# A Mamba block with a ternary FFN on one core: where rows load, which engine takes head 1's low weights, and three reordered steps

## What is computed

```python
zxbcdt = jnp.einsum('bld,ed->ble', u, W_in)
dt = jax.nn.softplus(zxbcdt[..., -NHEADS:] + dt_bias)
xBC = jax.nn.silu(xconv)                  # causal convolution over 4 positions of x, B and C
y = (Y_diag + Y_off).reshape(b, l, h, p)  # within a chunk, and from the state before it
yg = (y + x * D) * jax.nn.silu(z)
yn = yg * jax.lax.rsqrt(jnp.mean(yg * yg) + EPS) * norm_w
x = _layernorm(u + jnp.einsum('ble,de->bld', yn, W_out))
scale = jnp.mean(jnp.abs(w)) + EPS        # for W_up, W_gate and W_down
w_q = jnp.clip(jnp.round(w / scale), -1.0, 1.0) * scale
x = _layernorm(x + (silu(x @ w_up_q.T) * (x @ w_gate_q.T)) @ w_down_q.T)
```

## Time and profile before

| what | value |
|---|---|
| median of 3 runs | 1373.71 us (1372.25 to 1374.39) |
| the profiled execution's own time | 1370.55 us |
| its span | 1368.4 us |
| TensorE busy | 1331.5 us, 97% of the span |
| VectorE, ScalarE, GpSimd busy | 1046.1, 785.2 and 666.7 us |
| mean granted clock of TensorE | 0.997 of 2.4 GHz |

### The profile page before, as it was taken

The page is one execution under the profiler, slowest core; times in us unless marked ns, Lnnn a source line. Parts: engine busy times, 40 slices in busy tenths (PEclk is TensorE's granted clock), DMA queues, the critical chain, the costliest instruction groups (busy, mean ns, idle before and its releaser), DMA issues.

```text
span 1368.4 us, 24907 instructions
## 1 busy us (share of the span) xinstructions
PE 1331.5 (97%) x9318; PEld 867.0 (63%) x9318; DVE 1046.1 (76%) x1855; ACT 785.2 (57%) x1561; POOL 666.7 (49%) x640
## 2 busy tenths in 40 slices
PE   8987899999999999999999999999999999999998
PEld 5554455564655656556557767777777777777774
DVE  7985787886878868778786987777777767777675
ACT  6885475782865838748475544454545445454441
POOL 3883265573763836635356534343444435353331
PEclk9999999999999999999999999999999999999999
DMA  7536434362443643524546332223122322222001
GB/s 252 174 109 208 133 119 119 86 177 78 103 134 96 167 111 86 150 90 132 158 120 223 89 114 57 76 63 86 47 63 65 75 67 58 70 62 55 32 28 66
DMA packets 162776, 143.64 MB, mean 105 GB/s; under 512 B 101344, under 2 KB 123232, under 8 KB 161504
## 3 DMA queue, kind: packets, MB, share of 16 engines
q1 hardware_dynamic: 162656, 142.05, 36.2%
HBM read 99.93 MB, written 27.39 MB: 93 GB/s over the span
## 4 chain that ended last, share of the span: by engine, by line
PE 82%; DVE 8%; issue 4%; ACT 2%; POOL 2%; DMA 1%; SPq 0%; POOLq 0%; DVEq 0%; ACTq 0%
PE ring L935 20%; PE ring L1151 15%; PE ring L964 9%; PE p_turn L1131 7%; PE p_y L1131 7%; PE p_st L1131 6%; PE p_seg L1131 6%; PE p_y L1009 3%; PE p_y L1017 2%; PE p_st L999 2%; PE p_turn L989 2%; DVE acc L1831 1%; PE ring L1188 1%; DMA raw<-in_w_in 1%; POOL sq_sum L1643 1%
## 5 line engine op out<-in xcount | busy, mean ns | idle before, releaser
L935 PE MATMUL ring<-u_split,weights 128*128 128x512 f16 x1620 | 373.1, 380 | 0.5 <-DVE x_ch L1836 0.5
L935 PEld LDWEIGHTS ring<-u_split,weights 128*128 128x128 f16 x1620 | 154.3, 98 | 168.7 <-issue 4.1
L1739 POOL TENSOR_TENSOR xdt<-xdt 128x512 f32<-128x512 f32 x64 | 100.8, 1575 | 324.4 <-DVE xdt L2230 324.4
L964 PE MATMUL ring<-w_out,raw 128*128 128x512 f16 x672 | 147.3, 379 | 0.0
L1831 DVE SCALAR_TENSOR_TENSOR acc<-ring,taps,acc 128x511 f32<-128x511 f32 (+2 forms) x192 | 143.7, 749 | 4.5
L964 PEld LDWEIGHTS ring<-w_out,raw 128*128 128x128 f16 x672 | 65.8, 98 | 79.0
L1359 ACT ACTIVATE xdt<-p_turn,dts 128x128 f32<-128x128 f32 x256 | 72.9, 375 | 71.2 <-PE p_turn L989 71.1
L1635 POOL TENSOR_TENSOR raw<-yg,raw 128x512 f16<-128x512 f32 x64 | 78.8, 1232 | 66.0 <-ACT raw L1390 66.0
L1630 POOL TENSOR_TENSOR yg<-y_ch,z_ch 128x512 f32<-128x512 f32 x64 | 81.5, 1275 | 36.8 <-DVE y_ch L1966 36.8
L1368 ACT ACTIVATE p_seg<-cum_rows,cum 128x128 f32<-128x128 f32 x256 | 80.8, 389 | 6.9 <-DVE seg L1944 6.9
L1606 POOL TENSOR_TENSOR rstd<-var_e,exponent 128x1 f32<-128x1 f32 x32 | 19.6, 611 | 124.7 <-DVE var_e L1989 124.7
(11 more groups left out here) (400 smaller groups left out, 3264.2 us busy)
## 6 DMA issues: line engine op xcount, KB each, us to landing
cum_rows<-cum_dram SPq DMA_DIRECT2D x64, 256.0 KB, 4.1
quant<-in_w_ffn SPq DMA_DIRECT2D x24, 512.0 KB, 4.5
quant<-in_w_ffn SPq DMA_DIRECT2D x48, 256.0 KB, 4.7
cum_g<-cum_dram SPq DMA_DIRECT2D x64, 128.0 KB, 4.6
rows<-in_u_tok SPq DMA_DIRECT2D x32, 256.0 KB, 5.1
x_dram<-rows SPq DMA_DIRECT2D x32, 256.0 KB, 2.1
tern_ug<-quant SPq DMA_DIRECT2D x32, 256.0 KB, 3.2
u_raw<-in_u_t SPq DMA_DIRECT2D x7, 1024.0 KB, 7.7
```

The costliest lines, as they stand in the source:

```text
L935: mm = pe.matmul(bank_k[:, :], w_in[:, ws, k, col:col + P], us[:, par, k * T:(k + 1) * T], start=(i == 0), stop=(i == 3 * KD - 1))
L964: mm = pe.matmul(ring[b][:, :], ys[:, h, c * P:(c + 1) * P], w_out[:, ws, h, :], start=(h == 0 and ys is y_hi and ws == 0), stop=(h == H - ...
L1739: pool.tensor_tensor(tile_[:, 1, :, :], tile_[:, 0, :, :], tile_[:, 1, :, :], ALU.mult).then_inc(hid_ok, 1)
```

## The change

Five edits, in the order of the program:

- `POOL_HEADS` now holds head 1 too: its low weights are made by GpSimd, first of all its heads, and no longer by VectorE (`w_lo(2)`). The numbers that the semaphores wait for follow.
- VectorE's `dt_third` of the first block stands ahead of `cb_conv`.
- In slot (0, 3) ScalarE runs `x_dt` ahead of the tanh of z and of the exponential, and `wout_hi(1)` ahead of the convolution's tanh. ScalarE's sums of the even rows stand at other places: row 2 at the start of slot (0, 2) and none at its end, rows 4 and 6 in slot (0, 3), rows 8 and 10 in slot (1, 0), rows 12 to 18 in slot (1, 1), rows 20 and 22 in slot (1, 2) as before.
- SP issues four rows, not eight, before the store and the loads of the running sums of block 1; `load_u(2)`, the loads of the residual's input and the stores in slot (1, 2) move among the rows; VectorE's odd row sums in step 1 move a little.
- In every step `sum_squares` stands behind the dt projection and the tile of B and C, and `mean_square` behind `dt_first`. In the FFN's first round the residual of the last chunk moves behind two sums and a hidden product.

```diff
-POOL_HEADS = [2, 3, 7]
+POOL_HEADS = [1, 2, 3, 7]
...
-USES = ["x00", "x01", "x10", "x11", "ssq", "dt", "x20", "x21", "b", "cum", "x30", "x31", "cumt", "cb"]
+USES = ["x00", "x01", "x10", "x11", "dt", "ssq", "x20", "x21", "b", "cum", "x30", "x31", "cumt", "cb"]
...
-            rows_ = {(0, 1): (None, 0, None), (0, 2): (2, None, 4), (0, 3): (None, 6, 8), (1, 0): (None, 10, 12),
-                     (1, 1): (None, 14, 16, 18), (1, 2): (None, 20, 22)}
+            rows_ = {(0, 2): (2,), (0, 3): (None, 4, 6), (1, 0): (None, 8, 10), (1, 1): (None, 12, 14, 16, 18),
+                     (1, 2): (None, 20, 22)}
...
-                        sp.wait_ge(w_lo_ok, 3)
-                        sp.wait_ge(w_half_ok, 2)
+                        sp.wait_ge(w_half_ok, 1)
                         load_abs(0)
                         load_abs(1)
+                        sp.wait_ge(w_half_ok, 3)
                         load_wout(0)
...
+                    if p == 2 and is_at(n, 1):
+                        load_utok(0, 2)
+                        store_x1(0, 0)
+                        load_utok(0, 3)
+                        load_abs(18)
+                        load_abs(19)
+                        store_x1(0, 1)
+                        load_abs(20)
+                        load_abs(21)
+                        store_x1(0, 2)
+                        store_x1(0, 3)
+                        load_abs(22)
+                        load_abs(23)
+                        load_cum(n, par, 3)
...
                     if p == 1 and not first:
                         chunk_out(n - 1, 0)
-                        sum_squares(n - 1, turn_use(n, "ssq"))
                     if p == 1 and more(n):
                         dt_proj(n + 1, 1 - par, turn_use(n, "dt"))
                         cb_tile(n + 1, 1 - par)
                     if p == 1 and not first:
+                        sum_squares(n - 1, turn_use(n, "ssq"))
                         for c in range(1, C):
                             chunk_out(n - 1, c)
...
             dt_first(0, 0)
-            w_lo(2)
             dt_second(0)
+            dt_third(0, 0)
             cb_conv(0, 0, p_y[0])
-            dt_third(0, 0)
...
-                    if odd_rows(n, p, 0) is not None:
-                        magnitude(odd_rows(n, p, 0))
                     if p == 2 and more(n):
                         b_read(n + 1, 1 - par, turn_use(n, "b"))
                         dt_third(n + 1, 1 - par)
+                    if odd_rows(n, p, 0) is not None:
+                        magnitude(odd_rows(n, p, 0))
...
                     if p == 1 and not first:
                         normalise(n - 1, 0)
+                        if odd_rows(n, p, 2) is not None:
+                            magnitude(odd_rows(n, p, 2))
                         residual(n - 1, 1, ring[ring_bank("chunk", 1)])
...
-                    if attention_rest(t, q) in (0, 3):
+                    if attention_rest(t, q) == 0:
                         residual(NB - 1, attention_rest(t, q), p_down[attention_rest(t, q) % 2])
...
-                    if attention_rest(t, q) in (1, 2):
+                    if attention_rest(t, q) in (1, 2, 3):
                         residual(NB - 1, attention_rest(t, q), p_down[attention_rest(t, q) % 2])
```

More of the change, by code:

```diff
@@ L1508, in step @@
                         cb_tanh(n + 1, ring[ring_bank("cb", 0)])
[L1509 to L1510 removed]
+                    for when in (3, 4):
+                        if abs_rows(n, p, when) is not None:
+                            magnitude(abs_rows(n, p, when))
             run_steps(step)
@@ L2184, in step @@
                         continue
+                    if p == 1 and more(n):
+                        dt_first(n + 1, turn_use(n, "dt"))
                     if p == 1 and not first:
```

52 lines of the change are left out of this document (24 added, 28 removed).

## The result

| what | before | changed |
|---|---|---|
| median of the runs | 1372.99 us (4 runs, 1372.25 to 1374.39) | 1358.94 us (4 runs, 1356.77 to 1359.32) |
| ratio to before | 1 | 0.9893, interval 0.9876 to 0.991 |
| profiled execution, its span | 1370.55 us, 1368.4 us | 1359.32 us, 1357.7 us |
| TensorE busy | 1331.5 us | 1329.9 us |

The change makes the kernel 14.05 us faster by the medians; 17.7 were forecast. The executions also differ in the clock: seven runs of the kernel before, taken beside e1_start_back, had mean granted clocks of 0.989 to 0.997, its profiled one 0.997, and all four runs of the changed kernel 0.998.

What follows compares the result with a forecast made beforehand. TensorE, busy 97% of the span, bounds the kernel, so only its idle time can be won. Terms sum to 17.65 us off 1370.55, giving 1352.9; plus 3.16 for the median, 1356.0; 8 in 10 within 1351.5 to 1364.0.

Steps and rivals of the forecast that it cites:

- the likeliest case's own range: Whole kernel: the forecast case alone, given a chance of 0.50, was to take 1353.5 to 1358.5 us.
- the start: 0 to 24 us: GpSimd's subtraction for head 1 holds VectorE's small steps until 18.1 us; 2.0 us lost, bounds 0 and 2.8.
- the rows: First slots of step 1: row 10 lands at 98 to 99 us, its wait nearly goes; gain 10.0, bounds 8.5 and 10.3.
- the last chunk: Beside the FFN: VectorE's residual moves behind two sums TensorE waits for; gain 1.7 us, bounds 0.5 and 1.75.
- the gain on `da`: Slot after the chunks of step 1: moving VectorE's sum of row 21 behind dt removes 1.07 us before `da`; gain 1.05.
- the 0.77 for the next multiplication: Start: GpSimd's multiplication might hold the small steps too, another 0.77 us on `dts`; only the bound of 2.8 us lost.
- Slot (0, 3) and slot (1, 0): Earlier x_dt shortens one wait and grows the next to 1.1, gain 1.1; w_out copies fill idle time, gain 1.45.
- The price of the low clock: First slots of step 1: 1.6 us at 1.2 GHz after the long idleness was to go, within the gain of 10.0.
- Chunks and the carry: Step 1's carry wait goes, gain 3.5; later sum of squares gains 1.5 over steps, loses 0.65 before step 1's chunk 3.
- The signs that were named: Profile: `da` wait above 0.8 us, x_ch's towards 1.5; no xdt wait over 1.2, no carry wait; cum store before 85.
- rival (b): Steps 0 and 1: new waits that the old ones covered, 4 to 8 us, total 1360 to 1364 us; chance 0.22 or 0.18: 0.18.
- no slice of the clock below 9: Sign for 60 to 110 us: the changed profile's clock row was to show no slice under 9.

Runs made afterwards that it cites:

- e1_start_back: Changed kernel with both start edits undone: VectorE makes head 1's low weights again, dt's third part stands behind the convolution of B and C; median 1358.07 us.
- e10_three: Changed kernel with e2_dve_sub, e4_root_late and e6_u_late joined; median 1353.62 us, ratio to before 0.9859.
- e2_dve_sub: Changed kernel with only head 1's low weights back on VectorE, dt's third part still ahead of the convolution of B and C; median 1358.66 us.
- e11_four: As e10_three, with ScalarE's tanh of z and exponential behind the second x_dt of slot (0, 3); median 1356.28 us, ratio to before 0.9876.
- e6_u_late: Changed kernel with the 1 MB load of u for block 2 issued behind rows 10 and 11; median 1355.82 us, ratio to before 0.9874.
- e7_ssq_back: Changed kernel with sum_squares and mean_square back in their old places; one execution, 1362.26 us.
- e9_row21_back: Changed kernel with VectorE's sum of row 21 back ahead of b_tok's copy and dt's third part; one execution, 1357.33 us.
- e4_root_late: Changed kernel with GpSimd's power step for the last residual moved behind the two hidden products of its round; median 1357.56 us.
- e12_with_row21: As e10_three, with VectorE's sum of row 21 moved back as in e9_row21_back; median 1352.80 us, ratio to before 0.9849.
- e3_bc_first: Changed kernel with only the convolution of B and C back ahead of dt's third part, head 1's low weights still on GpSimd; median 1361.60 us.
- e5_row10_behind: Changed kernel with ScalarE's sum of row 10 moved behind the first x_dt and decays of slot (1, 1); median 1361.50 us.

## Why the prediction was right, and where it wasn't

The time lies in the range, 2.9 us above the value named and 0.4 above the likeliest case's own range. Part of that is luck. The sum was made for the profiled execution, 1352.9 us, and the profiled one took 1359.32, 6.4 more. The forecast then added 3.16 us, by which the median of the kernel before lay above its profiled execution, and in the changed kernel the median lies 0.4 below. This took back 3.5 us of the miss. Most mechanisms held; the start and the rows were mis-sized, the last chunk came with the other sign, the gain on `da` was credited to the wrong edit, and one cost had no term.

**The start.** Forecast -2.0, measured -4.1. The hold was read rightly from the earlier trace rows, and `dt_q` was let go at 18.16 where 18.1 was said. The sum failed in two terms. Behind the subtraction it counted 0.85 us for the four steps, with the 0.77 for the next multiplication only as a bound: that bound was the case (`da` 0.99 us), as `dts` in the earlier trace rows had shown. And it had no term for the clock, though it had one for slot (1, 1): 1.4 us here, 1.6 and 2.8 in two others of the seven executions with this start, none in four. What lets it fall stays open: it did so without GpSimd's pair too (e10_three, 1.6 us) and with the start of the kernel before (e1_start_back, 1.1 us). The Trainium skill (SBUF — State Buffer, Who interferes with whom) has the lock held for the whole instruction; for GpSimd's subtraction the traces agree (held to its end in each case), for its multiplication they don't: VectorE's steps got through 1.1 us after it began, of 2.8. e2_dve_sub and the two kernels with a late piece show that it is the overlap that costs and not the order.

**Slot (0, 3) and slot (1, 0).** 1.04 for 1.1, with the second wait grown to 1.20 as was said, and 1.92 for 1.45. e11_four shows that those 1.20 us can't be had by moving the same two steps again.

**The rows.** Forecast +10.0, measured +7.9 here and 4.2 to 7.9 in the other kernels of this order. The failed step is the one that let row 10 land 4 to 5 us after its issue. It took that from loads that ran alone, and didn't price that the change issues u's megabyte ahead of the row; the prediction said of SP's moves only whom they wait for. The issue itself came at 98.14 and not near 94: 1.7 us of that is lead that the earlier stretches had not brought, and the rest ScalarE's own list, which had the sum of row 8 at 96.97. ScalarE was ready for row 10 at 102.71, not at 98.5, so the late issue alone would have cost nothing; the 6.5 us behind it did. e6_u_late gives 9.91 us, with at most 4.5 us of landing. The price of the low clock, 1.6 in the forecast, was 1.2.

**Chunks and the carry.** Chunk 3's 1.02 us (said: about 1.0) and the carry's 3.6 (said: 3.5) hold, with no wait in front of chunk 3 in the other steps. e7_ssq_back prices the move of the sum of squares at 0.5 to 0.95 us with all, where 1.5 - 0.65 = 0.85 was the forecast. (One word of the count is wrong: 241.9 us, where chunk 3 begins in the earlier trace rows, is two thirds into the row of 15.70, not one.)

**`da` in slot (1, 2).** The 1.07 us went, as forecast, but not by the step that was credited. e9_row21_back puts the sum of row 21 back and the wait stays away: VectorE had been late there from its 5.34 us on u_tok, in the earlier trace rows, and the repaired loads took both away. The gain was counted to the wrong edit, and the edit's own price, the load of row 23 a microsecond later and 0.9 us in slot (1, 3), was not seen at all. What the prediction asked of rows 12 to 21, who waits for the load behind this sum, it didn't ask of this one.

**The last chunk.** Forecast +1.7, measured -0.5. The failed step: "Behind it now come only half a hidden tile and the down weights' loads". It followed VectorE's list alone. GpSimd's power step for this residual had stayed ahead of two hidden products in GpSimd's list, so that moving its producer back moved them back as well. e4_root_late gives 1.5 of the 2.2 us.

**The signs that were named.** No wait on the carry in front of the states, the store of cum at 83.8 us, chunk 3's wait and the pair near 780 us came as said, and so did a wait for `da` near 19 us above 0.8 (1.66). The wait for the first `x_ch` did not grow towards 1.5 us: it is 0.73, and 2.02 us stand on `darg` ahead of it, which no line of the forecast had. A wait on `xdt` of 2.03 us and a row for which ScalarE waits 1.92 were not to come: by its own words the prediction is wrong there, and the outcome lies between the forecast and its rival (b), new waits under the old ones. The sign "no slice of the clock below 9" was too coarse, since a slice of the page is 34 us long and the low stretches last 3.

## What to carry to other kernels

When a step is moved later on one engine, follow its result to the next engine's list and look what stands behind the instruction that waits for it; VectorE's move took away waits of 0.90 and 0.85 us and brought one of 2.20, of which 1.5 were GpSimd's power step. A load's time to landing holds only for the traffic it was read in: look at which transfer the change puts ahead of it. And when two edits could each remove a wait, the sum must credit the cause once and still price what the other edit delays.

## What was not expected of the hardware

VectorE's small steps are let go about 1.1 us after the beginning of a GpSimd multiplication by a constant (2.8 us, 128 x 1024), in each of these cases: a multiplication at 13.12 and `dt_n` done at 14.20, at 18.56 and `da` done at 19.63, at 14.11 and `dt_m` (one SBUF operand only) done at 15.21, at 19.08 and `dt_s` done at 20.17. A GpSimd subtraction of two operands holds to its end (18.11 and 18.16; 19.13 and 19.16). VectorE's multiply-adds that read PSUM ran at 0.75 to 0.8 us each beside either.

TensorE's clock fell to 1.2 GHz behind the waits of the start in ten of the thirteen kernels with the changed rows, at one of two places 5 us apart, and in e2_dve_sub, e6_u_late and e9_row21_back not at all. It is not tied to GpSimd's hold: e10_three, e11_four and e12_with_row21 have the start of e2_dve_sub and fell. At the earlier place a later wait took it up where there was one (e4_root_late, e7_ssq_back) and it cost 1.1 us where there was none (e1_start_back, e3_bc_first); at the other it cost 1.4 to 2.8 us. Runs of one kernel differ with it: the four of e5_row10_behind took 1357.99 us at a mean granted clock of 1.000, and 1361.39 to 1361.75 at 0.996 and 0.997. Where it fell in the runs that were not profiled, no trace shows.
